# Gated two-layer Flamingo block on one core: one exponential per half, no second copy of the router rows, and TensorE's attention part written out

## The reference, cut to what matters

```
n   = layernorm(x)
q,k,v = n @ w_qkv.T                       # 16 heads of width 8
k,v = concat(context k,v ; own k,v)       # 64 context keys and 64 own keys
p   = softmax(q * scale @ k.T)            # per sequence and head: 64 x 128
x   = x + tanh(g) * (p @ v @ w_proj.T + b_proj)
h   = layernorm(x)
expert = argmax(h @ gate_w)               # one of 8 experts for each token
x   = x + tanh(g) * (shared_swiglu(h) + swiglu_of_expert(h * sigmoid(max logit)))
```

## Time and profile before

| what | value |
|---|---|
| median of 3 runs | 490.39 us (489.52 to 491.38) |
| span of the profiled execution, first to last instruction | 490.0 us |
| PE busy | 443.7 us (91%), 6871 matmuls |
| DVE busy | 366.8 us (75%) |
| POOL busy | 319.4 us (65%) |
| ACT busy | 277.8 us (57%) |

### The profile page before, as it was taken

One profiled execution on the slowest core, in us unless ns is written; L12 is line 12 of the kernel. 1 busy time (PEld: TensorE's weight loads), 2 busy tenths in 40 slices (PEclk: granted clock), 3 DMA queues, 4 the chain that ended last, 5 costly groups with the idle time before them and its releaser, 6 DMA issues. The chain is left out here.

```text
span 490.0 us, 20510 instructions
## 1 busy us (share of the span) xinstructions
PE 443.7 (91%) x6871; PEld 349.2 (71%) x6872; DVE 366.8 (75%) x1201; ACT 277.8 (57%) x775; POOL 319.4 (65%) x780
## 2 busy tenths in 40 slices
PE   5789999989999999997987999987997799899998
PEld 3456677756766666774666988864655799898997
DVE  3668999978898989944768666545766678788984
ACT  2468899877988888764234545434233434444431
POOL 3845765567777777767723666577825899898630
PEclk9889999998999999989999999998999699999999
DMA  7941231111111110100245776631000011111001
GB/s 232 413 152 41 48 36 27 26 31 40 28 32 33 30 36 22 37 20 18 76 131 158 228 227 216 222 121 37 18 5 13 16 46 33 46 37 37 23 23 33
DMA packets 37394, 37.38 MB, mean 76 GB/s; under 512 B 20440, under 2 KB 31504, under 8 KB 36816
## 3 DMA queue, kind: packets, MB, share of 16 engines
q0 software_dynamic: 7552, 20.20, 12.9%
q1 hardware_dynamic: 29200, 16.06, 11.9%
q10 hardware_dynamic: 576, 0.26, 0.2%
HBM read 24.82 MB, written 7.86 MB: 67 GB/s over the span
## 5 line engine op out<-in xcount | busy, mean ns | idle before, releaser
L979 DVE TENSOR_REDUCE negm<-PS 128x4 f16<-128x512 f32 x128 | 81.9, 681 | 0.4
L716 ACT ACTIVATE pexp<-PS 128x512 f32<-128x512 f32 x128 | 69.4, 595 | 6.4 <-PE PS L1383 5.8
L1725 PE MATMUL PS<-w,vp 128*128 128x128 f32 x512 | 63.3, 277 | 0.0
L1725 PEld LDWEIGHTS PS<-w,vp 128*128 128x128 f32 x512 | 60.6, 194 | 0.0
L1396 PEld LDWEIGHTS PS<-pexp,vp 128*32 128x32 f32 x2048 | 34.5, 113 | 26.4 <-issue 20.5
L1396 PE MATMUL PS<-pexp,vp 128*32 128x64 f32 x2048 | 50.3, 230 | 0.3
L1619 PE MATMUL PS<-xsT,wst 128*128 128x128 f32 x320 | 44.4, 282 | 3.0 <-DVE stack L1217 1.3
L1619 PEld LDWEIGHTS PS<-xsT,wst 128*128 128x128 f32 x320 | 38.8, 191 | 7.3 <-issue 5.0
L581 POOL DMA_INDIRECT sorted_x<-VALL,posu x32 | 33.3, 1040 | 13.4 <-issue 7.6
L611 POOL DMA_DIRECT2D wst<-in_rt_gate_up_dram x40 | 21.5, 538 | 29.2 <-PE PS L1619 19.9
L1310 DVE TENSOR_TENSOR vp<-PS,xnT 128x1024 f32<-128x1024 f32 x32 | 38.6, 1205 | 0.8 <-PE PS L1702 0.8
(11 more groups left out here) (246 smaller groups left out, 1254.5 us busy)
## 6 DMA issues: line engine op xcount, KB each, us to landing
wst<-in_rt_gate_up_dram POOLq DMA_DIRECT2D x40, 256.0 KB, 3.5
xs<-sorted_x SPq DMA_DIRECT2D x40, 64.0 KB, 2.8
sorted_y<-YS POOLq DMA_DIRECT2D x40, 64.0 KB, 3.0
out_dram<-X SPq DMA_DIRECT2D x32, 64.0 KB
X<-in_x_dram SPq DMA_DIRECT2D x1, 1536.0 KB, 8.2
CK<-in_ctx_k_dram SPq DMA_DIRECT2D x1, 1536.0 KB, 12.2
CV<-in_ctx_v_swapped_dram SPq DMA_DIRECT2D x1, 1536.0 KB, 16.6
rdn<-in_rt_down_dram POOLq DMA_DIRECT2D x1, 1024.0 KB, 10.6
```

Source lines behind the costliest of these rows:

```text
L716: nc.scalar.activation(pexp[:, j, :], PS[:, 2 + j % 2, :], ACT.Exp).then_inc(S["exped"], 1)
L979: dve.tensor_reduce(negm[:, a.par, :, j], PS[:, j % 2, :].rearrange("p (g k) -> p g k", g=G), AX.X, ALU.max, negate=True).then_inc(S["maxe ...
L1725: nc.tensor.matmul(PS[:, 6 + y.par, 0:D], z[:, y.par, e, :], w1[:, e * D:e * D + D], start=(e == 0), stop=False)
```

## The change

Four edits, all in the attention part.

1. ACT takes one exponential of 128x1024 over banks 2 and 3 where it took two of 128x512. It waits until both banks have their scores. The semaphore `exped` counts halves and no longer chunks, and PE's waits are rewritten for that.
2. ACT copies the router's turned rows once, into `XNT`. The router's logits on PE read `XNT`; the tile `xrT` and ACT's wait for the logits are gone.
3. PE's attention part is written out in full (`looped=False`). The loops of ACT, DVE and SP stay.
4. In PE's step `scores_by_key(b, 1)` stands ahead of `average(b, 0)`.

```diff
--- before.py
+++ after.py
@@ -247,7 +247,6 @@
         halves = sb("halves", [P, 2])
         ve2 = sb("ve2", [P, 2])
         xr = sb("xr", [P, 2, D])
-        xrT = sb("xrT", [P, 2, P])
         str_ = sb("str_", [P, 2, 6])
         rstdr = sb("rstdr", [P, NT])
         mv2 = sb("mv2", [P, 2, 2])
@@ -694,7 +693,7 @@
 
         @block.scalar
         def _(act):
-            credit(act, ("xnT_kept", 1), ("exped", 4), ("on_kept", 1), ("hi_ready", 1), ("v_kept", 1),
+            credit(act, ("xnT_kept", 1), ("exped", 2), ("on_kept", 1), ("hi_ready", 1), ("v_kept", 1),
                    ("max_kept", 1), ("o_kept", 1), ("ctx_hi", 1), ("q_kept", 1), ("ctx_kept", 1),
                    ("r_xnT_kept", 1))
             quad_credit(act, ("k_faded", 1))
@@ -710,10 +709,10 @@
                                twice_over(CK[:, f.cols(D)].rearrange("p (h d) -> p h d", h=H)))\
                     .then_inc(S["ctx_hi"], 1)
 
-            def exp_chunk(b, j):
-                act.wait_ge(S["scored_t"], b.done(4, j))
-                act.wait_ge(S["averaged"], b.freed(4, j, back=4))
-                nc.scalar.activation(pexp[:, j, :], PS[:, 2 + j % 2, :], ACT.Exp).then_inc(S["exped"], 1)
+            def exp_half(b, half):
+                act.wait_ge(S["scored_t"], b.done(4, 2 * half + 1))
+                act.wait_ge(S["averaged"], b.freed(4, 2 * half + 1, back=4))
+                nc.scalar.activation(pexp[:, 2 * half:2 * half + 2, :], PS[:, 2:4, :], ACT.Exp).then_inc(S["exped"], 1)
 
             def step(stage):
                 l, f, s, w, b, n, c, k = (stage(i) for i in (0, 1, 2, 4, 5, 7, 9, 12))
@@ -731,8 +730,7 @@
                         act.wait_ge(S["on_turned"], n.done())
                     nc.scalar.copy(mT[:, w.par, :], bank16(6)[0:H, 7 * P:8 * P]).then_inc(S["max_kept"], 1)
                 if b:
-                    exp_chunk(b, 0)
-                    exp_chunk(b, 1)
+                    exp_half(b, 0)
                 if f:
                     act.wait_ge(S["qkv_done"], f.freed())
                     act.wait_ge(S["xnT_done"], f.done())
@@ -746,8 +744,7 @@
                     nc.scalar.copy(qc[:, s.slot], bank16(5)[:, 0:512].rearrange("p (g t) -> p g t", g=G))\
                         .then_inc(S["q_kept"], 1)
                 if b:
-                    exp_chunk(b, 2)
-                    exp_chunk(b, 3)
+                    exp_half(b, 1)
                 if s and turned_on_pe(s):
                     act.wait_ge(S["ctx_turned"], s.done())
                     last = nc.scalar.copy(ctx_half(s.slot), by_seq(bank16(6)[:, 0:512]))
@@ -769,9 +766,7 @@
                         act.wait_ge(odd_stack, 2)
                     ctx_hi(l)
                 if c:
-                    act.wait_ge(S["r_routed"], c.freed())
                     act.wait_ge(S["r_xnT_done"], c.done())
-                    nc.scalar.copy(xrT[:, c.par, :], PS[:, 6, 2 * P:3 * P])
                     nc.scalar.copy(XNT[:, c.cols(P)], PS[:, 6, 2 * P:3 * P]).then_inc(S["r_xnT_kept"], 1)
                 if b:
                     act.wait_ge(S["o_turned"], b.freed())
@@ -1374,7 +1369,7 @@
 
                 if half == 0:
                     pe.wait_ge(shift_placed[b.par], 16 * (b.pair + 1))
-                pe.wait_ge(S["exped"], b.freed(4, 2 * half + 1, back=2))
+                pe.wait_ge(S["exped"], b.freed(2, half, back=1))
                 for seq in range(2):
                     for g in range(G):
                         for hg in (2 * half, 2 * half + 1):
@@ -1390,7 +1385,7 @@
                 if j == 0:
                     pe.wait_ge(S["v_spread"], b.done())
                     pe.wait_ge(S["o_kept"], b.freed(back=1))
-                pe.wait_ge(S["exped"], b.done(4, j))
+                pe.wait_ge(S["exped"], b.done(2, j // 2))
                 for seq in range(2):
                     for g in range(G):
                         last = nc.tensor.matmul(PS[32 * g:32 * g + 32, 7, j * P + SEQ * seq:j * P + SEQ * seq + SEQ],
@@ -1418,7 +1413,7 @@
                 if (c, i) == (0, 0):
                     pe.wait_ge(more_in, 16)
                     pe.wait_ge(S["maxed"], Tile(NT - 1).done(4, 3))
-                    pe.wait_ge(S["exped"], Tile(NT - 1).done(4, 3))
+                    pe.wait_ge(S["exped"], Tile(NT - 1).done(2, 1))
                 pe.wait_ge(S["r_xnT_kept"], Tile(CT * c + CT - 1).done())
                 back = 2 if c < EARLY else 1
                 pe.wait_ge(S["h_acted"], Tile(c).freed(2, i, back=back))
@@ -1521,7 +1516,7 @@
                     pe.wait_ge(S["on_kept"], m.done())
                 if rl:
                     at = 3 * P + rl.slot * E
-                    nc.tensor.matmul(PS[:, 6, at:at + E], xrT[:, rl.par, :], gatew[:, 0:E], start=True, stop=True)\
+                    nc.tensor.matmul(PS[:, 6, at:at + E], XNT[:, rl.cols(P)], gatew[:, 0:E], start=True, stop=True)\
                         .then_inc(S["r_routed"], 1)
                 if m and m.turn is None and m.n == NT - 1:
                     shared_lift(0, 0, 1)
@@ -1553,8 +1548,8 @@
                     pe.wait_ge(S["normed"], f.done())
                     nc.tensor.transpose(PS[:, 4, 0:P], xn[:, f.par, :], identf).then_inc(S["xnT_done"], 1)
                 if b:
+                    scores_by_key(b, 1)
                     average(b, 0)
-                    scores_by_key(b, 1)
                 if a:
                     scores_for_max(a, 1)
                 if f:
@@ -1596,7 +1591,7 @@
                     average(b, 2)
                     average(b, 3)
 
-            walk(pe, NT, 13, step, drain=shared_in_drain)
+            walk(pe, NT, 13, step, drain=shared_in_drain, looped=False)
 
             pe.wait_ge(texp_ready, 1)
             pe.wait_ge(late_ready, 4)
```

## The result

The kernel after takes 495.12 us (median of 6 runs, 493.54 to 506.33), the kernel before, run beside it, 491.42 us (6 runs, 489.52 to 498.39). The ratio is 1.0089, 95% interval 1.0052 to 1.0125: slower, by 2.6 to 6.1 us. The profiled execution took 495.49 us with a span of 493.9 us, so 1.6 us lie between a span and the time of the same execution. The 0.39 us that the prediction used lay between a span and the median of other executions. Ratios here leave out runs disturbed by a lower clock of the chip; medians have them in.

What follows compares the result with a forecast made beforehand. PE bounds the early tiles and the drain, the ring of DVE and POOL the stretch from about 80 us; 1.45 + 0.15 + 0.25 + 0.1 + 0.85 - 0.45 - 0.35 + 1.2 = 3.2 us, giving 493.3 us, range 489.3 to 496.8.

Steps and rivals of the forecast that it cites:

- The stalls: PE idle for the merged exponential ahead of the second scores: 0.29 us a tile at tiles 1 to 5, less later.
- rival D: Merged exponential dearer than by column, near 1.19 us: 0.17 us more at some 15 tiles, +2.5 us; 0.19 with Rival A.
- The duration near 50 us: PE's step in the early tiles, near 50 us, goes from 5.45 to 5.75 us, released by ACT's exponential.
- The fetches in the loop's stretch: 119 to 195 us: about 15 packets of PE's written-out code delay router scatters; 1.2 us, bounds 0 to 4.5.
- three tight scatters: Looped stretch: three scatters with 0.2 us of slack, each one chance in three to meet a fetch, at 1 to 1.5 us.
- Back edges: PE's loop ends at 119, 144 and 169 us: only the one at 119 us gains, 0.35 us.
- The drain: After the last new tiles PE is the chain again: stalls cost 0.85 us, the single copy gains 0.45 us.
- The single copy: ACT's one copy of router rows: nothing in the loop; 0.15 x 3 = 0.45 us gained in the drain.
- Rival A: Fetches hit all three tight scatters and a few others: +4 to +6 us, 494.8 to 498; chance 0.19 with rival D.
- my own forecast: Whole kernel: PE's stalls and some fetch collisions with scatters, 492 to 494.8 us; chance 0.45.
- Rival C: Faster: back edges, shorter drain and new group order gain; 489 us, or 487 without PE's stalls; chance 0.12.
- Rival B: PE's stalls are there but the fetches miss the scatters: 492.4 us, or 491; chance 0.24.

Runs made afterwards that it cites:

- h1: Kernel before with only the merged exponential and the swap (second scores ahead of average 0); loop and both router copies kept; ratio 1.0007.
- e3: Kernel before with only the second scores moved ahead of average 0; two exponentials and the loop kept; ratio 0.9957.
- e1: Kernel before with only PE's attention part written out; 492.90 us, ratio 1.0009.
- f3: Kernel before with one copy of the router rows and PE written out; two exponentials and old order kept; 495.48 us, ratio 1.0074.
- f5: Kernel after with average 0 ahead of the second scores again, the exponential still merged; ratio 1.0102.
- h4: Kernel after with only the single copy undone: ACT copies the router's rows twice again; ratio 1.0117.
- f4: Kernel after with two exponentials of 128x512 again, the second scores still ahead of average 0; ratio 1.0142.
- e6: Kernel after with 48 small matmuls more in PE's warm-up, moving the places of its instruction fetches; 494.73 us, ratio 1.0072.
- i1: f3 with SP reading two counts more ahead of its transfers of zeros, so that ACT issues first; ratio 1.0118.
- g2: Kernel after with POOL's 1/sqrt for the first layer norm moved to the top of its step; 488.82 us, ratio 0.9931.

## Why the prediction was right

It said 493.3 us and slower as the likeliest; 495.12 us lies in its range. The forecast was 2.9 us above the kernel before (490.39), and the ratio measured says 4.4 (2.6 to 6.1). It was right for the mechanisms and partly by luck, since errors of 1 to 2 us cancel.

- *The stalls.* Predicted 1.45 + 0.15 + 0.25 + 0.1 = 1.95 us by tile 28, most of it before 81 us. Measured 1.41 us in the kernel after, 1.17 in h1, 1.11 in e3, and -0.53 and -0.09 in e1 and f3, which keep the old order and two exponentials. Shown in place and size, and by f5's timeline for the merge without the swap. The exponential lasts 1030 ns over all 64, the sum had 1025; rival D falls.
- *The duration near 50 us.* Predicted a step of 5.75 us, released by ACT; measured 5.75.
- *The fetches in the loop's stretch.* "I take 1.2 us; bounds 0 and 4.5", less 0.35 for a back edge: 0.85. Measured +3.17 from 126 to 190 us. This is the mis-sized term. Of the three tight scatters (128.00, 155.78 and 181.54 us) one was hit, as the one chance in three says, and it cost 1.58 us. The other 1.59 us came from scatters that I had given 0.8 to 1.5 us of slack and counted as mostly hidden: POOL waited for three of them. From their landings the slack was 0.64, 0.91 and 0.93 us (3.74 - 2.30 - 0.80, 3.60 - 2.30 - 0.39, 3.92 - 2.30 - 0.69), and a hit delays by 1.0 to 1.7. In e1, h4, f3, f4 and f5 the same stretch cost 0.95 to 1.64 us. That is the size predicted, but in f3 and f4 no tight scatter was hit and all of POOL's waits there were for the others, so the agreement is in part luck. e6 had one tight scatter hit and lost 5.39 us, most of it by the clock.
- *The first scatters.* The sum has nothing for 81 to 126 us but 0.1 us, though the earlier trace rows show the wait of 1.52 us. The kernels whose first scatter POOL didn't wait for (after, e3, h1, f4, f5, e6) gain 1.2 to 2.1 us there; those in which it did (e1, f3, h4, i1) have -0.2 to +1.5. The granted clock from 80 to 120 us is 1.00 in each of the first, 0.91 to 0.96 in the second and 0.96 before, so the wait and the clock behind it come together. Missing term, -1.64 in the kernel after. It doesn't go with the writing out: e3 and h1, whose first scatter was free, have PE's loop as the kernel before has it, and around 105 us both kinds of program fetch.
- *Back edges.* The sum took one of three as worth 0.35 us, and 1.05 us for all of them by the Trainium skill (Runtime: NRT & Kernel Launch, Instruction fetch mechanics). That rule is for a branch whose target must be fetched, and no fetch on q8 ran at these edges, so the 1.05 us didn't follow from it. The three gaps, 0.28 to 0.30 us, are gone from the timelines of the kernel after and of e1, as predicted. A gain by it can't be seen: e1, whose only edit this is, has a ratio of 1.0009, and in the stretch from 81 to 126 us, where the paid one should be, its first scatter's wait is 0.35 us longer than before.
- *The drain.* Predicted 0.85 - 0.45 = +0.40. Measured +2.14 in the kernel after, but -0.65 in h4, -1.19 in e1, -1.08 in f3, +0.57 in h1, +3.39 in e3. These go with the granted clock from 205 to 225 us: 0.83, 1.00, 1.00, 1.00, 0.91 and 0.74; before had 0.91. (e6 and f5, at 0.91, have +0.51 and +1.95, so the clock isn't all.) So the term of work can't be told from one trace, and the clock is a large part of it. What puts the clock down in one kernel and not in the next stays open.
- *The single copy.* Priced at -0.45 us in the drain. h4 and after don't differ by more than their intervals; it brings or costs nothing that shows, apart from the 4 us of f3, f4 and i1, which have the ACT program with the stop.

Rival A (494.8 to 498 us) holds the measured time, at its lower end, and my own forecast (492 to 494.8) just misses it: the fetches hit harder than I took, and the gain by 126 us hid part of it. Rival C falls with the waits at L1378. Rival B describes h1.

Each whole is a sum of some eight chances of 1 to 4 us that no edit aims at. All kernels that are measurably slower have PE written out, and h1 and h4 differ in this edit alone: 1.0007 and 1.0117, with intervals that just don't overlap. That it is this edit is therefore likely, but not how: of the 2.6 us between their traces 1.37 lie in the stretch of the loop, and 3.6 between 81 and 126 us, where h4's first scatter was hit and the edit changes little, while the drain and the end give some back. And the same edit alone (e1, 1.0009) isn't slower, which is explained only in part, by a drain at full clock in its trace.

## What to carry to other kernels

- Look for the ring before pricing a stall or a late transfer. Here DVE waited for POOL's 1/sqrt in most steps, so a scatter late by more than 0.2 us (behind the row scaling) or 0.6 to 0.9 us (the others) was paid; a move of one block on POOL took the kernel after from 1.0089 to 0.9931.
- Writing a loop out isn't free when little is lost at its back edges: here it brought a 16 KB fetch each 5 to 6 us, and scatters that met one landed 0.7 to 1.7 us later. Whether the whole pays for it changes from kernel to kernel (1.0009 in e1, from 1.0007 to 1.0117 between h1 and h4). Count the waits with little slack, and expect the hits to change with any edit that changes the number of instructions.
- Merging two instructions into one that ends later is a loss at that place where the consumer could start on the first half, even if the merged one is cheaper (0.3 us a step here); the whole of h1, merge and swap with the loop kept, is not slower by what can be measured.

## What was not expected of the hardware

- With two fetches of ACT's own instructions inside it, a DMA issue took 2.00 to 2.41 us where it takes 0.43 us (three kernels with one ACT program). The stop cost 2.0 to 2.4 us, and the low clock of PE after the idle time that it made 1.7 us more.
- A single gap of 1.38 us on PE was followed by a granted clock of 0.52 and 0.80 over two windows of 10 us (e6), a gap of 1.89 us by 0.83 over one (after). One profile can be some 3 to 5 us off by the clock: from 35 to 81 us f5 and g2 lose 5.92 and 5.00 us at granted clocks of 0.86 and 0.84 from 30 to 80 us, the kernels with the same stalls at 0.97 to 1.00 lose 1.1 to 1.9.
